# Low parts of two masked pairs by transfers, paired shared low products, and a refinement layer in rounded parts

## The reference

```
logits = gelu(x @ w_r1 + b_r1) @ w_r2 + b_r2;  the two best of 8 experts per token, weights w
v = 0;  y = x
twice:
    ctx = [y, v]                                               (256 features)
    shared = gelu(ctx @ w_s1 + b_s1) @ w_s2 + b_s2             (64 hidden, 3*128 out)
    ctrl_e = gelu(ctx @ w1[e] + b1[e]) @ w2[e] + b2[e]         for both experts e of the token
    alpha, beta, gate = split(ctrl):  v' = sigmoid(alpha)*v - softplus(beta)*(y - mu)
                                      x' = y + 0.1*sigmoid(gate)*v'
    x_next, v = mix of the shared and the two experts' x', v'
    halt    = sigmoid(gelu(x_next @ w_h1 + b_h1) @ w_h2 + b_h2)
    refined = gelu(x_next @ w_f1 + b_f1) @ w_f2 + b_f2
    y = y + halt * refined * integration_weight
```

## Time and profile before

| | |
|---|---|
| median of 3 runs | 353.34 us (353.13 to 353.79) |
| profiled execution | 352.54 us, of which the span from first to last instruction 350.8 us |
| PE busy | 320.6 us (91%), 1498 products |
| DVE busy | 276.4 us (79%) |
| ACT busy | 194.8 us (56%) |
| POOL busy | 35.4 us (10%) |
| granted clock of TensorE, mean | 0.981 of full speed |
| steps 3 to 6 in the trace | begin at 206.8, about 230, 258 and 287 us; step 7 at 315.3 us |

### The profile page before, as it was taken

One profiled execution on the slowest core, in us unless ns is written; L12 is line 12 of the kernel. 1 busy time (PEld: TensorE's weight loads), 2 busy tenths in 40 slices (PEclk: granted clock), 3 DMA queues, 4 the chain that ended last, 5 costly groups with the idle time before them and its releaser, 6 DMA issues.

```text
span 350.8 us, 4318 instructions
## 1 busy us (share of the span) xinstructions
PE 320.6 (91%) x1498; PEld 225.9 (64%) x1498; DVE 276.4 (79%) x548; ACT 194.8 (56%) x307; POOL 35.4 (10%) x41
## 2 busy tenths in 40 slices
PE   4989999899898777896998999999999999999996
PEld 4654787445464454574675777777777777776763
DVE  0556767645757668969999999999997996999694
ACT  3500026285746274497778784866746846635743
POOL 0040020211111110709000100000000000000000
PEclk9989999999999679999999999999999999999999
DMA  7999930000000000000000100101000100000001
GB/s 266 421 429 298 325 153 0 0 2 2 0 2 0 0 1 2 0 0 2 1 0 0 33 0 2 30 0 30 2 1 0 32 1 0 32 0 0 32 0 60
DMA packets 11444, 18.91 MB, mean 54 GB/s; under 512 B 416, under 2 KB 8864, under 8 KB 10144
## 3 DMA queue, kind: packets, MB, share of 16 engines
q1 hardware_dynamic: 10848, 17.60, 14.5%
q0 software_dynamic: 576, 1.05, 1.8%
HBM read 16.55 MB, written 1.05 MB: 50 GB/s over the span
## 4 chain that ended last, share of the span: by engine, by line
PE 68%; DVE 15%; ACT 7%; issue 5%; POOL 2%; DMA 2%; SPq 0%; DVEq 0%; ACTq 0%; POOLq 0%
PE ps L1255 63%; DVE zz L860 3%; POOL lrs L381 2%; DVE lst L845 2%; PE ps L1352 2%; DMA ctxT<-in_ctxT 2%; PE ps L1331 1%; ACT hid L535 1%; DVE st L745 1%; ACT ring L483 1%; ACT L646 1%; DVE lmv L848 1%; DVE a L761 1%; PE ps L1437 1%; DVE kv L1144 1%
## 5 line engine op out<-in xcount | busy, mean ns | idle before, releaser
L1255 PE MATMUL ps<-hm_even,ew_hi 128*128 128x512 f32 (+1 forms) x160 | 51.0, 417 | 1.1 <-issue 1.1
L1255 PE MATMUL ps<-hm_odd,ew_hi 128*128 128x512 f32 (+1 forms) x164 | 51.6, 416 | 0.0
L1255 PEld LDWEIGHTS ps<-hm_odd,ew_hi 128*128 128x128 f32 (+1 forms) x164 | 28.7, 189 | 5.8 <-issue 0.5
L1255 PEld LDWEIGHTS ps<-hm_even,ew_hi 128*128 128x128 f32 (+1 forms) x160 | 27.9, 188 | 6.3 <-issue 1.2
L535 ACT ACTIVATE hid<-ps,pB 128x512 f32<-128x512 f32 x32 | 21.6, 687 | 13.4 <-PE ps L1255 12.8
L1255 PE MATMUL ps<-hm_odd,ew_lo 128*128 128x512 f32 (+1 forms) x80 | 28.3, 391 | 0.0
L1255 PE MATMUL ps<-hm_even,ew_lo 128*128 128x512 f32 (+1 forms) x80 | 28.3, 390 | 0.0
L860 DVE TENSOR_SCALAR zz<-ps,lmv,lrs 128x128 f32<-128x128 f32 x48 | 16.4, 404 | 9.4 <-POOL lrs L381 9.2
L381 POOL TENSOR_TENSOR lrs<-lve,mhalf 128x4 f32<-128x4 f32 x12 | 12.2, 1017 | 106.0 <-DVE lve L850 106.0
L1255 PE MATMUL ps<-x_hi,w1x_hi 128*128 128x512 f32 x40 | 18.9, 474 | 4.3 <-ACT ring L503 2.2
L945 DVE SCALAR_TENSOR_TENSOR ring<-ring,pB,hid 128x1024 f32<-128x1024 bf16 x16 | 20.5, 1282 | 2.0 <-ACT hid L535 1.3
(11 more groups left out here) (291 smaller groups left out, 739.4 us busy)
## 6 DMA issues: line engine op xcount, KB each, us to landing
ring<-in_fc1b SPq DMA_DIRECT2D x4, 1024.0 KB, 17.8
ring<-in_fc2a SPq DMA_DIRECT2D x4, 1024.0 KB, 8.9
packC<-in_packC SPq DMA_DIRECT2D x1, 1152.0 KB, 9.3
pB<-in_packB SPq DMA_DIRECT2D x1, 1141.5 KB, 10.1
ctxT<-in_ctxT SPq DMA_DIRECT2D x2, 512.0 KB, 6.7
xtok<-in_xtok SPq DMA_DIRECT2D x1, 1024.0 KB, 9.4
xT<-in_xT SPq DMA_DIRECT2D x1, 1024.0 KB, 11.4
a<-in_fc1a SPq DMA_DIRECT2D x1, 1024.0 KB, 13.4
```

Source lines behind the costliest of these rows:

```text
L1255: return pe.matmul(out, lhsT, rhs, start=start, stop=stop)
```

## The change

1. **Low parts by transfers.** In steps 1, 2 and 3 (`MOVED`) the low parts of pairs 2 and 3 are no longer subtracted by DVE. DVE writes the high part negated; SP copies it to the place of the low part; POOL then adds `hm` to it in an accumulating transfer. PE multiplies these high parts by negated weights (`ew2_neg`, `ew2_low_neg`, two ACT copies in the prologue). The order in `hidden_masked(1)` is new: the masks and high parts come before `state_split`. The constant row of `r1` moves to another tensor and its memset to a later place.
2. **Paired shared low products.** From step 2 on the `ws2_lo` product of the second group is computed in BETA's row tiles, in the lower half of the rows, beside BETA's own in the upper half. For this ACT makes three gelus of the shared tile in place of two: an unrounded and a rounded one of partitions 64 to 127, a rounded one of partitions 0 to 63.
3. **Second layer in rounded parts.** For steps 4, 5 and 6 (`SPLIT`) f2 is six rounded products in place of two plain ones. ACT makes a rounded copy of each of the two gelus, DVE a low part (`refine_low`, 128x1024, behind `halt_low`); `wf2` is split once, in step 4.

```diff
+        MOVED = (1, 2, 3)
...
+        def negated(s, j):
+
+            return s in MOVED and j >= 2
+
+        def low_ready(engine, s, j):
+
+            if negated(s, j):
+                engine.wait_ge(sem(f"hlo_{j}"), 16 * (MOVED.index(s) + 1))
+            else:
+                engine.wait_ge(sem("hlo"), hlo_at(s, j))
...
+        SPLIT = range(NCH, STEPS - 1)
+        PAIRED = 2
...
+        def hsu_at(s):
+
+            return s + 1 + max(0, s + 1 - PAIRED)
...
+            for n, s in enumerate(MOVED):
+                for j in (2, 3):
+                    sp.wait_ge(sem("hhi"), hhi_at(s, j))
+                    sp.dma_start(low_of(s, j).bitcast(F), high_of(s, j).bitcast(F)).then_inc(sem("low"), 16)
+                    sp.wait_ge(sem("low"), 16 * (2 * n + j - 1))
...
+                if n == 2:
+                    pool.wait_ge(sem("w1_ps"), 1)
+                    pool.wait_ge(sem("lrs"), 2)
+                    pool.memset(r1[32:33, :, :], 1.0).then_inc(sem("r1one"), 1)
+                    pool.wait_ge(sem("r1one"), 1)
...
+            for n, s in enumerate(MOVED):
+                for j in (2, 3):
+                    pool.wait_ge(sem("low"), 16 * (2 * n + j - 1))
+                    pool.dma_start(low_of(s, j), hm[j % 2], accum_op=ALU.add).then_inc(sem(f"hlo_{j}"), 16)
+                if s == 1:
+                    weigh(2)
...
-                        act.activation(hs, hid_bank(s, HT), ACT.Gelu, bias=W("bs1")).then_inc(sem("hs"), 1)
-                        if s >= 2:
+                        if s >= PAIRED:
 
                             act.wait_ge(sem("part_ps"), group(s - 1, 0))
-                        act.activation(hsh[:, s % 2, :], hid_bank(s, HT), ACT.Gelu, bias=W("bs1"))\
-                            .then_inc(sem("hsu"), 1)
+                            out, half = hid_bank(s, HT), slice(64, 128)
+                            act.activation(hsf[half, s % 2, :], out[half], ACT.Gelu, bias=W("bs1")[half])\
+                                .then_inc(sem("hs"), 1)
+                            act.activation(hs_hi[s % 2][half, :], out[half], ACT.Gelu, bias=W("bs1")[half])\
+                                .then_inc(sem("hsu"), 1)
+                            act.activation(hsh[0:64, s % 2, :], out[0:64], ACT.Gelu, bias=W("bs1")[0:64])\
+                                .then_inc(sem("hsu"), 1)
...
+                if t == 2:
+
+                    act.wait_ge(sem("bp"), 1)
+                    act.wait_ge(sem("ew2_lo"), 2)
+                    for out, w in ((ew2_neg, ew2_hi), (ew2_low_neg, ew2_lo)):
+                        act.activation(out[:, :], w[:, 2 * 3 * D:].bitcast(F), ACT.Copy, scale=-1.0)\
+                            .then_inc(sem("ew2_neg"), 1)
...
+                    if s in SPLIT:
+                        act.activation(fh_hi[:, j, :], bank[7 - j], ACT.Gelu, bias=W("bf1", j, j + 1))\
+                            .then_inc(sem("fhi"), 1)
                     act.activation(fh[:, j, :], bank[7 - j], ACT.Gelu, bias=W("bf1", j, j + 1))\
                         .then_inc(sem("fhg"), 1)
...
-                act.activation(h1, bank[7], ACT.Gelu, bias=W("bh1")).then_inc(sem("h1f"), 1)
+                act.activation(h1[32:64], bank[7][32:64], ACT.Gelu, bias=W("bh1")[32:64]).then_inc(sem("h1f"), 1)
                 act.activation(h1s, bank[7], ACT.Gelu, bias=W("bh1")).then_inc(sem("h1"), 1)
...
+                if s == NCH:
+                    act.wait_ge(sem("hm"), (HT - 1) * (s + 1))
+                    act.activation(wf2_hi, W("wf2"), ACT.Copy).then_inc(sem("wf2"), 1)
...
-                    dve.wait_ge(sem("hlo"), HT * s - (j - 1))
+                    low_ready(dve, s - 1, 2 if j == 2 else 3)
...
+            def high(s, j):
+
+                if s >= 2:
+                    dve.wait_ge(sem("part_ps"), group(s - 1, 0))
+                dve.wait_ge(sem("hm"), (HT - 1) * s + j)
+                if negated(s, j):
+                    dve.tensor_scalar(high_of(s, j), hm[j % 2], -1.0, None, ALU.mult).then_inc(sem("hhi"), 1)
+                else:
+                    dve.tensor_copy(high_of(s, j), hm[j % 2]).then_inc(sem("hhi"), 1)
...
-                if s >= 2:
-                    kept(s, 1)
+                if s == 1:
+                    kept(s, 2)
+                    high(s, 2)
+                    lower(s, 1)
+                    kept(s, 3)
+                    high(s, 3)
+                    lower(s, 0)
+                    state_split(s + 1)
+                    slot_masks(s + 1)
+                    shared_halves(s)
+                    return
+                kept(s, 1)
                 kept(s, 2)
+                if s in MOVED:
+                    high(s, 2)
                 if next_state:
                     state_split(s + 1)
                 lower(s, 0)
                 lower(s, 1)
                 kept(s, 3)
-                lower(s, 2)
+                if s in MOVED:
+                    high(s, 3)
+                else:
+                    lower(s, 2)
                 if s <= 2:
                     slot_masks(s + 1)
                 shared_halves(s)
-                lower(s, 3)
+                if s not in MOVED:
+                    lower(s, 3)
...
+                if s >= PAIRED:
+                    dve.wait_ge(sem("hsu"), hsu_at(s) - 1)
+                    dve.tensor_tensor(hsh[half, s % 2, :], hsf[half, s % 2, :], hs_hi[s % 2][half, :].bitcast(F),
+                                      ALU.subtract).then_inc(sem("hsl"), 1)
...
-                dve.wait_ge(sem(f"xsum_{NCH - 1}"), 16)
+                dve.wait_ge(sem("xsum"), 16 * NCH)
...
+            def refine_low(s):
+
+                dve.wait_ge(sem("fhg"), 2 * s + 2)
+                dve.wait_ge(sem("fhi"), 2 * (s - SPLIT[0]) + 2)
+                dve.tensor_tensor(fh_lo[:, :, :], fh, fh_hi[:, :, :].bitcast(F), ALU.subtract).then_inc(sem("flo"), 1)
...
+                if s == NCH:
+                    dve.wait_ge(sem("wf2"), 1)
+                    dve.tensor_tensor(wf2_lo, W("wf2"), wf2_hi.bitcast(F), ALU.subtract).then_inc(sem("wf2"), 1)
...
+                if s - 1 in SPLIT:
+                    refine_low(s - 1)
...
                     pe.wait_ge(sem("hsl"), s + 1)
+                    pe.wait_ge(sem("hsu"), hsu_at(s))
                     last = mm(sh, ws2_hi[:, o], h, start=first, stop=not first)
...
-                    mm(hi, w_hi[bot, :], m[bot, 1, 0, :], start=False, stop=not first)
-                    return mm(sh, ws2_lo[top, o], h[top, :], start=first, stop=not first)
+                    last = mm(hi, w_hi[bot, :], m[bot, 1, 0, :], start=False, stop=not first)
+                    if paired and part == parts(s)[1]:
+                        return last
+                    if paired and rows_last:
+
+                        pe.wait_ge(sem("squash"), 2 * n)
+                        pe.wait_ge(sem("hsu"), hsu_at(s))
+                    last = mm(sh, ws2_lo[top, o], h[top, :], start=first, stop=not first)
+                    if paired and rows_last:
+                        p = parts(s)[1]
+                        mm(bank[3 * (n % 2)], ws2_lo[bot, p * D:(p + 1) * D], hs_hi[s % 2][bot, :], stop=False)
+                    return last
...
-                    pe.wait_ge(sem("hlo"), hlo_at(s, j))
+                    low_ready(pe, s, j)
                     out = hi if k else lo
-                    mm(out, weights(ew2_hi, j), m[:, 0, i, :], start=rows_last and j == 1, stop=False)
-                    mm(out, weights(ew2_lo, j), m[:, 0, i, :], start=False, stop=False)
+                    if negated(s, j):
+                        pe.wait_ge(sem("ew2_neg"), 2)
+                        w_hi, w_lo = weights(ew2_neg, j - 2), weights(ew2_low_neg, j - 2)
+                    else:
+                        w_hi, w_lo = weights(ew2_hi, j), weights(ew2_lo, j)
+                    mm(out, w_hi, m[:, 0, i, :], start=rows_last and j == 1, stop=False)
+                    mm(out, w_lo, m[:, 0, i, :], start=False, stop=False)
                     last = mm(out, weights(ew2_hi, j), m[:, 1, i, :], start=False,
...
+                if s in SPLIT:
+                    pe.wait_ge(sem("wf2"), 2)
+                    pe.wait_ge(sem("flo"), s - SPLIT[0] + 1)
                 for j in range(2):
-                    last = mm(bank[7], W("wf2", j * 128, (j + 1) * 128), fh[:, j, :],
-                              start=j == 0, stop=j == 1)
+                    w = slice(j * 128, (j + 1) * 128)
+                    if s in SPLIT:
+                        mm(bank[7], wf2_hi[:, w], fh_hi[:, j, :], start=j == 0, stop=False)
+                        mm(bank[7], wf2_lo[:, w], fh_hi[:, j, :], start=False, stop=False)
+                        last = mm(bank[7], wf2_hi[:, w], fh_lo[:, j, :], start=False, stop=j == 1)
+                    else:
+                        last = mm(bank[7], W("wf2")[:, w], fh[:, j, :], start=j == 0, stop=j == 1)
                 last.then_inc(sem("f2_ps"), 1)
                 if s + 3 < STEPS:
```

(18 more changed lines are left out.)

69 lines of the change are left out of this document (40 added, 29 removed).

## The result

The changed kernel takes 360.28 us (median of six runs, lowest 359.46) against 353.24 us; the ratio of the runs is 1.0166, 95% interval 1.0119 to 1.0212. It is slower, by 7.0 us between the medians, where 4.74 had been forecast; 360.28 lies inside the range of 354.6 to 361.7, but above the 356.8 to 359.4 of the forecast itself. One of the six runs took 365.96 us at a mean granted clock of 0.963, and the ratio leaves it out. Beside the experiments the median of the kernel before lay between 352.72 and 355.14 us, so that the 7.0 is good to a microsecond or two. The profiled execution took 360.6 us, 8.06 more than that of the kernel before. The head of its page: PE is busy longer, DVE shorter, ACT 9.6 us longer, and the clock row has two low slices that it did not have: the nineteenth of forty, just short of the middle, and one near the end.

The account below looks back on a forecast made before the run. PE was taken to set the time from step three's middle to step seven, DVE after it. −0.19 + 2.90 − 0.69 + 0.15 + 1.26 + 1.26 + 0.05 = +4.74 us on 353.34 gave 358.1; range 354.6 to 361.7.

Parts of the forecast that it names:

- rival C: Steps one to three: low-part transfers come late and PE waits at its third pair; 361.5 us at 17 us a pair; chance 0.11.
- third gelu: Shared tile's added gelu on ACT delays PE by 0.58 us in each of steps one to five: +2.90 us.
- refine_low: Added DVE subtraction: free in step four, +1.26 us behind halt_low of step five, +1.26 behind that of step six.
- The sixth: Step six: the shared tile's added gelu makes DVE's rr start later, +0.15 us.
- Rival B: Shared tile's added gelu is hidden, so 2.90 and 0.15 us go: 355.0 us; chance 0.14.
- rival A: Steps three to seven: PE's own work decides, added DVE and ACT work fits beside it; faster, 351.3 us; chance 0.12.
- The slots of the pair: PE loses one 512-column product a step by pairing low products; counts in steps three to five: −0.69 us.
- Rival D: Paired low products run one after the other, 0.69 us not gained: 358.8 us; inside the forecast's 0.60, no separate chance.
- The transfers: Steps one to three: 9 us a pair, landing within 12 us of the high part, PE never waiting: 0 us.
- The rule that spoke against the part: DVE's fp32 copies lock GpSimd out of a shared port: each accumulation up to 2.5 us later, sum unchanged.
- becomes a wait for ACT: hidden(2): of PE's 2.02 us wait for slot_masks 0.19 is gained, the rest turns into waiting for ACT's gelus.

Follow-up runs that it names:

- changed again: The changed kernel, same code, profiled a second time to see where half-clock stretches fall: 360.74 us.
- e4: Changed kernel with ten products that compute nothing needed in each of two PE idle times, in hidden(2) and ahead of refine_a of step seven: 360.22 us, ratio 1.0159.
- e8: Changed kernel with products that compute nothing needed in all PE idle times behind 124 us: 359.36 us, ratio 1.0136.
- e3: Changed kernel with part 1 undone (all low parts by DVE, old order in step one, no negated weights): 361.67 us, ratio 1.0190.
- e1: Changed kernel with part 2 undone (two gelus of the shared tile, no paired low product): 357.48 us, ratio 1.0100.
- e2: Changed kernel with part 3 undone (second layer in full precision, no refine_low, no wf2 split): 356.99 us, ratio 1.0110.
- e7: Kernel before with part 2 alone, h2 and step one's expansion issued one tile later: 355.48 us against 354.75 beside it, ratio 1.0003.
- e9: Kernel before with products that compute nothing needed in its PE idle times behind 124 us: 355.02 us, ratio 1.0018.
- before again: The kernel before, unchanged, profiled a second time to see where half-clock stretches fall: 352.43 us.
- e10: Changed kernel with h2 and step one's expansion one tile later, and part 3 in step four alone: 356.87 us against 355.14 for the kernel before, ratio 1.0061.
- e6: Kernel before with part 1 alone (parts 2 and 3 undone): 354.69 us against 352.72 beside it, ratio 1.0024.
- e5: Changed kernel with h2 (and step one's expansion) issued one tile of control products later: 360.02 us, ratio 1.0175.

## Why the prediction was right, and where it was not

Right: slower, within the range, and by the causes named. That the number came out inside the range is in part luck: it lies 0.9 us above the forecast's own 356.8 to 359.4 (its bounds, added up, give 357.0 to 359.2), in room that was left for rival C, late transfers, and that case did not come. The intervals of the changed kernel at full clock (changed again, e4, e8) against the terms of the sum:

```
               said    measured   measured by
E to R         +0.39    +0.59     -0.14 part 1 (e3), +0.70 third gelu (e1)
R to X         +3.04    +3.12     2.10 part 2 (e1), 1.13 refine_low (e2)
X to L         +1.31    +1.32     1.23 refine_low (e2)
L to end        0       +0.37     part 1 (e3: 0.36)
sum            +4.74    +5.40
ahead of E      0       +0.47     one execution; see below
half clock      -       +2.17     0.69 in E to R, 1.48 in X to L
total          +4.74    +8.04     of the 8.06 between the profiled executions
```

**The third gelu** was right in its mechanism, its places and its signs: h2 starts 0.06 us behind its end, PE waits for it five times, in steps two to six, and that of step one is the 0.86 us of "issue" at 171.17, 0.70 before. The size was near. From the start of the second gelu (269.52) to that of the third (270.21) it is 0.69, where 0.58 had been taken from one gelu of the same kind behind another: the two before overlap by 0.09 us, the third, in the other half of the partitions, by nothing. PE pays less than that in steps two to five, 0.61 (2.56 in place of 1.95), since h2 takes 0.34 us behind its wait where it took 0.43; in step one it pays 0.70 (e1). The five places come to 3.1 us in place of 2.90. The sixth is as said: `rr` in step six starts 0.15 us later (21.88 for 21.73 us behind refine_a of step five). Rival B falls with e1, and rival A with it: PE's own slots alone, as e7 has them, gave 0.37 us up to X and no measurable difference in the time.

**The slots of the pair** were gained: e7, with the gelu under cover, has 0.82 us less up to step six (three slots are 0.69; the late h2 may have a part in it). The two low products start together, at 326.17. Rival D falls.

```profile
326.17 0.39 PE L1378 MATMUL ps<-hsh,ws_lo 64*128 64x512 f32 x1
326.17 0.39 PE L1378 MATMUL ps<-hs_hi_odd,ws_lo 64*128 64x512 f32 x1
```

**refine_low** cost 1.13 and 1.23 us for 1.26 each, in the two places named, and the first of the three cost nothing. f2 and h2 of step seven take 1.61 us ("1.6"), 0.35 less than before as said. (Only the split into 1.52 and 0.43 was misread: the 1.52 holds a wait for the gelu. In step seven, where none is, h2 followed f2 after 1.32, at 316.59, and took 0.64.) In the same way refine_a waited 2.48 us ("over 2"), halt_low to the last state took 11.02 us to its end where 11.2 had been said.

**The transfers** came as said: 10.5 us behind the high part in step one (within 12), and PE waited for none. Rival C falls. The estimate of 9 us for a pair was near: from the issue of the last copy to the landing it took 8.0 us in steps two and three (copy 3.1, accumulation 4.6) and 10.4 in step one. The rule that spoke against the part (the Trainium skill, SBUF — State Buffer, § SBUF: two separate sides: DVE's fp32 copies lock GpSimd out while it writes descriptors) shows itself in 0.2 us at most in the issues: that at 157.84, amid DVE's fp32 work, took 1.07 us, the others 0.85 to 0.95, two of these amid such work too. The transfer issued at 157.84 landed after 5.8 us in place of 4.6, but SP's copy beside it was as much slower (5.5 for 3.0), so the cause of that is not settled. No issue fell into one of DVE's casts, so this doesn't refute the rule; it never decided here.

**The term that was missing** is the clock. The prediction did not weigh it: it wrote that the wait of 2.02 us "becomes a wait for ACT", and that PE waits over 2 us at refine_a, and priced both by their length. The products behind an idle time can run at half clock. That was 2.17 us of the profiled execution, none of it in the same two places in the second profile of the same code, which had its stretch ahead of E. In the medians the part of it is not settled: 7.0 us between them, 5.4 by the terms, so some 1.6 for the clock and the head of the kernel together, about as much as the median of the kernel before moves. Joining two idle times (2.02 and 0.65 us, before) into one of 2.65 was rated a gain of 0.19; the gain is there (0.14), but what it does to the clock was not weighed. No run shows that the joined wait is the reason; e1 had it and kept 1.00.

**Ahead of E** the changed kernel was 0.47 us later. e7 and e9, built on the kernel before without part 1, have w1 at 39.6 and 39.8 us where the kernel before has it at 38.7 and 38.4, and the changed kernel at 39.3 (39.28 in e3, without part 1); what lies ahead of it varies by up to 1.8 us between executions (e2: 40.2). From w1 to E the changed kernel takes 119.3 us, the kernel before 119.5 and 119.7. So the 0.47 lies wholly ahead of w1, and the two copies of negated weights, behind it, cost nothing that shows.

**Open** is why part 1 adds 0.37 us behind the last state; the traces show where. From DVE's last output to the landing of the last store it is 1.9 us in all kernels. From that landing to the end of the kernel it is 0.39 us in the five profiles without the transfers (before, before again, e3, e7, e9) and 0.73 in the eight with them, and the two last semaphore instructions of POOL start 0.08 us apart in the first and 0.42 in the others. What in part 1 makes POOL slower there, no run shows. Open too is the remainder of e10, and with it whether the changed prologue draws more stretches at half clock than the old one: among 17 runs beside e10 six of the kernel before took 352.2 to 352.8 us, and none of e10's twelve took under 354.2; e6, with part 1 alone, shows the same, and e7, without it, had three of ten under 353.

## What to carry to other kernels

Ask of every instruction added to an engine with slack who stands in another engine's queue at the moment it ends: ACT had slack enough for the third gelu and still PE paid 0.6 to 0.7 us for it five times, until the product that waited for it stood one tile later in PE's queue. Before a wait of TensorE is moved, split or joined, price the products behind it at both clocks. Where executions of one kernel differ by more than the change, cut the profiles at common events and compare only intervals whose clock row is full.

## What the runs showed of the hardware

- The same code has its stretches at 1.2 GHz in other places from one execution to the next, most of them 3 to 7 us long (in e3 one of 10, from 135 to 146 us), and worth 0.7 to 2.7 us in work that sets the time (e5, X to L: 22.90 for 20.21). Of 19 executions of the kernel before beside e7 to e9 the eight with a mean granted clock of 0.981 took 352.2 to 352.9 us, the eleven below it 353.9 to 357.7. The mean is not all: beside e10 one of six at 0.981 took 355.1.
- Behind products that compute nothing the clock was 1.00 wherever they stood (e4, e8, e9, one profile each); it was 1.00 in two of these places without them too (e1, changed again). In e4, with some idle times filled, a stretch stood behind the next one left.
- A gelu of one half of the partitions behind one of the other half doesn't overlap with it: they start 0.69 us apart, those of the same half 0.59 (six of each in the changed kernel).
- A copy of 512 KB from tile to tile landed 3.0 us after SP's issue, an accumulation as large 4.6 us after POOL's; where the two ran side by side (157.84 and 158.38), the accumulation took 5.8 and the copy 5.5.
- On PE, f2 and the h2 behind it took 1.61 us in step seven with f2 in six rounded products, and 1.96 with two full-precision ones. By the starts f2 itself is no longer in full precision (1.32 for 1.38); the product behind it costs 0.64 in place of 0.23.
